# Four graph layers in one kernel: a comparison in another form, and a call moved inside a sum

## The reference

```python
# first layer: graph convolution
deg  = segment_sum(1, dst);  dinv = rsqrt(deg)
msg  = h[src] * dinv[src] * dinv[dst]
x   += h + relu(segment_sum(msg, dst) @ W_gcn @ W1 + b1) @ W2 + b2
# fourth layer: attention on edges, per pair (i, o) of 16 x 16
w_m  = (efeat @ W_msg  + b_msg ).reshape(E, 16, 16)
w_a  = (efeat @ W_attn + b_attn).reshape(E, 16, 16)
e1, e2 = w_m * h[src][:, :, None], w_a * h[src][:, :, None]
attn = exp(e2 - segment_max(e2, dst)) / segment_sum(exp(...), dst)
x   += segment_sum(e1 * attn, dst).sum(axis=1)
```

## Time and profile before

| | us |
|---|---|
| median of three runs | 9471.54 |
| profiled execution | 9465.25 |
| its span | 9463.5 |
| busy TensorE / VectorE | 7645.1 / 7338.7 |
| busy GpSimd / ScalarE | 6896.2 / 4606.7 |

### The profile page before, as it was taken

One profiled execution on the slowest core, in us unless ns is written; L12 is line 12 of the kernel. 1 busy time (PEld: TensorE's weight loads), 2 busy tenths in 40 slices (PEclk: granted clock), 3 DMA queues, 4 the chain that ended last, 5 costly groups with the idle time before them and its releaser, 6 DMA issues. The chain is left out here.

```text
span 9463.5 us, 135509 instructions
## 1 busy us (share of the span) xinstructions
PE 7645.1 (81%) x35152; PEld 4283.9 (45%) x35152; DVE 7338.7 (78%) x11881; ACT 4606.7 (49%) x7496; POOL 6896.2 (73%) x6335
## 2 busy tenths in 40 slices
PE   3777774999999728888888888578888888888884
PEld 3666653555555415555555555333333333333331
DVE  6666653777777738888888888588888998988987
ACT  4666663667667416565655665323333333333333
POOL 6777776766666567777777777378777777777774
PEclk9888886777777659999999999789999999999997
DMA  4222211111111111111111111122222222222223
GB/s 147 55 52 53 55 46 36 42 41 40 42 41 40 34 17 32 31 27 31 31 27 31 31 31 21 18 62 72 77 72 71 72 71 75 75 71 72 71 74 99
DMA packets 498923, 493.19 MB, mean 52 GB/s; under 512 B 180303, under 2 KB 396134, under 8 KB 497959
## 3 DMA queue, kind: packets, MB, share of 16 engines
q1 hardware_dynamic: 298823, 371.60, 11.6%
q0 software_dynamic: 199904, 119.78, 9.1%
HBM read 240.96 MB, written 249.95 MB: 52 GB/s over the span
## 5 line engine op out<-in xcount | busy, mean ns | idle before, releaser
L2485 POOL DMA_INDIRECT attn_got<-tab,attn_line x1760 | 2152.3, 1223 | 648.7 <-issue 511.2
L1945 POOL DMA_INDIRECT sheaf_got<-tab,sheaf_idx x1612 | 1712.7, 1062 | 490.0 <-issue 472.5
L2538 PE MATMUL attn_q<-attn_X,ident 128*128 128x512 f32 x3520 | 1799.3, 658 | 1.8 <-DVE attn_X L2710 1.8
L2034 PE MATMUL sheaf_acc<-sheaf_hot_hi,sheaf_wide 128*128 128x392 bf16 x6696 | 1361.4, 346 | 272.1 <-DVE sheaf_hot_hi L2237 270.2
L1469 POOL DMA_INDIRECT nnconv_got<-tab,nnconv_idx x1116 | 1100.0, 986 | 456.0 <-issue 322.8
L1167 POOL DMA_INDIRECT gcn_got<-tab,gcn_idx x868 | 1018.9, 1174 | 301.4 <-issue 275.4
L2671 DVE TENSOR_TENSOR attn_T<-attn_w,attn_got 128x1024 f32<-128x1024 f32 x880 | 1035.0, 1218 | 246.4 <-PE attn_w L2529 206.6
L2538 PEld LDWEIGHTS attn_q<-attn_X,ident 128*128 128x128 f32 x3520 | 699.9, 210 | 1136.6 <-issue 1136.6
L2615 ACT COPY attn_S<-attn_q 128x512 f32<-128x512 f32 x440 | 255.9, 582 | 1624.4 <-PE attn_q L2545 1624.4
L2034 PEld LDWEIGHTS sheaf_acc<-sheaf_hot_hi,sheaf_wide 128*128 128x128 bf16 x6696 | 657.2, 106 | 809.2 <-issue 481.0
L2529 PE MATMUL attn_w<-src_hi 32*128 32x512 f32 x3520 | 586.5, 738 | 437.6 <-DVE attn_T L2671 436.7
(11 more groups left out here) (502 smaller groups left out, 13931.2 us busy)
## 6 DMA issues: line engine op xcount, KB each, us to landing
sums<-attn_S SPq DMA_DIRECT2D x110, 1024.0 KB, 4.2
tops<-attn_S SPq DMA_DIRECT2D x110, 512.0 KB, 2.9
attn_got<-tab,attn_line POOLq DMA_INDIRECT x1760, 2.6
sheaf_got<-tab,sheaf_idx POOLq DMA_INDIRECT x1612, 2.4
gcn_key<-src_key SPq DMA_DIRECT2D x62, 384.0 KB
gcn_blk<-src_blk SPq DMA_DIRECT2D x62, 384.0 KB
nnconv_got<-tab,nnconv_idx POOLq DMA_INDIRECT x1116, 2.4
nnconv_key<-src_key SPq DMA_DIRECT2D x62, 256.0 KB, 3.1
```

Of the source, the lines that this page charges most:

```text
L1945: e.indirect_dma_start(out=got[at.b][:, j, D:D + T2], out_offset=None, in_=tab[2], in_offset=indices(idx[at.b], j)).then_inc(s_got[half][a ...
L2034: mm = e.matmul(pacc[k][:, 0:HH], wide[at.b][half][:, part, col, :], hot[:, k * HH:(k + 1) * HH], start=False, stop=False, skip_group_chec ...
L2485: e.indirect_dma_start(out=got[at.b][:, 4 * q + n, :], out_offset=None, in_=tab[3], in_offset=indices(ids[:, q, n, :], D + 2)).then_inc(s_ ...
L2538: e.matmul(to, ident[:, :], X[:, q, :, n, :], start=n == 0, stop=False)
```

## The change

A bank of PSUM is set to one at the start of the first convolution, and `chosen` compares with `scalar_tensor_tensor` instead of `tensor_scalar`: the comparison's result is multiplied by that bank. In attention `quad_sum` takes a function that it calls after its third identity matmul; for quad 0 of a block this function is the call of `matrices(at.plus(2), 0)`, which stood behind the whole sum.

```diff
+            pone = ps("gcn_one", [P, 512], banks)
...
                     ch.do(e.memset(pcnt[:, 0:C], 0.0))
+                    ch.do(e.memset(pone[:, :], 1.0))
...
                         for n in range(NC):
-                            hit = e.tensor_scalar(hot[q][:, n, :], key[at.b][:, g, :], key_of[:, n:n + 1], None, ALU.is_equal)
+                            hit = e.scalar_tensor_tensor(out=hot[q][:, n, :], in0=key[at.b][:, g, :], scalar=key_of[:, n:n + 1],
+                                                         in1=pone[:, :], op0=ALU.is_equal, op1=ALU.mult)
                         hit.then_inc(s_hot, 1)
...
-                    def quad_sum(at, q):
+                    def quad_sum(at, q, between=None):
...
                         for n in range(4):
                             e.matmul(to, ident[:, :], X[:, q, :, n, :], start=n == 0, stop=False)
+                            if between and n == 2:
+                                between()
...
-                        quad_sum(at, 0)
-                        if at.k < NBQ - 2:
-                            matrices(at.plus(2), 0)
+                        quad_sum(at, 0, (lambda: matrices(at.plus(2), 0)) if at.k < NBQ - 2 else None)
```

## The result

The kernel after takes 9212.98 us (median of three, 9211.11 to 9216.05) against 9471.54: ratio 0.9727, 95% interval 0.9705 to 0.9749. The profiled execution took 9216.05 us, 249.2 less than the one before; the other 9.4 us of the medians' difference lie in which execution was profiled.

A forecast was written before the change was run, and what follows sets the result against it. GpSimd's gathers bound the first convolution; in attention VectorE and TensorE wait for each other. Profiled 9465.25 us less 73 (first convolution) and 86 (attention) gives 9306, plus 6.3 to the runs' median: 9312 us, range 9260 to 9410.

The forecast's parts named there:

- Who bounds the first convolution, and what the new form costs: First convolution: GpSimd's gathers set the 20.70 us period; new comparisons step 0.66 us, seven take 4.62, 1.76 more.
- The sum there: First convolution: first copy 6.5 us later, then 61 periods of 19.4 us, ending at 1347 against 1420: -73 us.
- The two loops: First convolution, per block after the change: VectorE's loop at 18.9 us and GpSimd's gathers at 19.1 us.
- the surcharge: First convolution: a period of 19.4 us taken, above loops of 18.9 and 19.1, because each perturbs the other.
- Attention's place of the gain and its cap: Attention: matrices 1.77 us earlier remove VectorE's 1.23 us wait; the second matrices cap the period's fall at 0.89 us.
- the slack of 0.89 us: Attention: second matrices usable at 7422.55 us, used by VectorE at 7423.44; all that the period can fall.
- Attention's sum: Attention: 0.8 us taken for each of 108 blocks, -86 us, bounds 0 and 140; slow groups after the idle stretch unchanged.
- GpSimd's 27.6 us in attention as a bound: Attention: GpSimd's instructions with their issue need 27.6 us per block; its pace limits the gain to 1.3 us a block.
- The lock rule: First convolution: skill page's full block of GpSimd beside two-port VectorE; a rival blocking scan and digits had 20.1 us, chance 0.08.
- The range: Whole kernel: 9260 to 9410 us, drawn past the rival in which attention gives nothing (9398 us, chance 0.12).
- the prediction's own bounds: Largest gains allowed per stage: -100 us in the first convolution (period 18.95 us), 140 us in attention (GpSimd's pace).

The follow-up runs named there:

- x8: The kernel after, with three filling matmuls into a bank nobody reads in TensorE's idle stretch in attention; 9198.83 us, ratio 0.9716.
- x12: The kernel before, with one filling matmul in TensorE's idle stretch in attention, order of calls unchanged; 9438.29 us, ratio 0.9967.
- x5: The kernel after, with the moved call one matmul later, after the fourth identity matmul; 9215.65 us, ratio 0.9736.
- x3: The kernel after, with the ones in SBUF and not in a PSUM bank; 9513.49 us, ratio 1.0052.
- x7: The kernel before, with three filling matmuls in TensorE's idle stretch in attention, order of calls unchanged; 9298.22 us, ratio 0.9822.

## Why the prediction was wrong

- *Who bounds the first convolution, and what the new form costs.* Right. The step from one comparison to the next is 658 ns (0.66 taken), seven take 4.70 us, 1.84 more than before (1.76 taken), the first copy comes 6.7 us later (6.5), and gathers beside the new form are at 0.95 us.
- *The sum there.* Wrong in size: -99.5, not -73. "The two loops, 18.9 and 19.1 us, nearly tie, and each perturbs the other, so I take 19.4": they hardly perturb each other; the period is 19.07. Without the surcharge, 61 x 0.33 = 20 us of the 26 missing are there; the rest is the last period, 12.1 us, in which ScalarE, which waited 6.93 us for the last gathers before, finds them done.
- *Attention's place of the gain and its cap.* Right: the wait for the first matrices goes, the slack of 0.89 us limits it, and a like block is 0.82 us shorter. In the kernel after VectorE's second multiplications start 1.31 us after their matrices in the mean, 1.27 being the least; before it was 2.21, so the slack is used up. VectorE's own work is as near: with the clock up (x8) the period is still 27.33 us, against 27.40 in the short blocks of the kernel after.
- *Attention's sum.* This is the step that failed: "TensorE's idle stretch of 3.89 falls to about 3.0 us, still long, so I leave the slow groups after it as they are". They did not stay: blocks with over 6 us at the low clock fell from 43 of 94 to 4 of 98, worth 0.6 us a block, 65 us. It was a term of the sum set to nought without bounds. Of the two misses this is the one that decides: with the first convolution as measured and attention as forecast the time would be some 9285 us, inside the range. Why the second low stretch stays away in this order is open: x12 shows that the idle stretch's length alone doesn't do it, and x5 that the exact place of the call doesn't matter.
- *GpSimd's 27.6 us in attention as a bound.* Wrong: the period went below it, to 27.45. A gather's mean length fell from 1223 to 1178 ns, so such a pace is not a constant of GpSimd; that VectorE's work falls otherwise beside it is the likely reason, not a tested one.
- *The lock rule.* The Trainium skill's page "SBUF — State Buffer", section "Who interferes with whom", puts a full block beside two-port modes, and also between a VectorE instruction with two SBUF inputs and a GpSimd instruction that reads SBUF. Neither the old comparisons, 1.28 us for a gather, nor the kernel after, whose period was 19.07 and not 20.1, show a block over the whole row of instructions. It came in x3, beside an operation with two tensors in SBUF: 5.00 us beside 4.72, for 33 of 552 gathers, while most beside the same comparisons took 1.02 us.
- *The range.* It ended at 9260 for want of a term for the clock. It was also narrower than the prediction's own bounds, -100 and -140 us, which end at 9231; the measured 9213 is below these too, since attention alone gave 153.5 us, more than its bound of 140.

## What to carry to other kernels

Where GpSimd issues gathers all the time, look at where both tensors of VectorE's neighbouring operations lie: the form with a second tensor cost VectorE 0.66 us a comparison instead of 0.41, in a bank or out of it, and still won with that tensor in a bank of PSUM; the same operation with both in SBUF lost all of it. Where TensorE idles once per block, price the slow matmuls after it as a term of their own, with a bound that they go: a few matmuls into a bank that nobody reads test that in one run. Two edits that remove the same wait don't add up, so ask what stands behind it first.

## What the runs showed of the hardware

A gather issued by GpSimd lasted 0.95 us beside comparisons with one tensor in PSUM; with both in SBUF most lasted 1.02 us, and 33 of 552 some 5.0 us, the length of all seven. The digits' operation slowed a gather to 1.8 us with both tensors in SBUF and not at all with one in a bank and in f32, at an equal length of its own (1.48 us). In attention the granted clock alone was worth 170 us: after an idle stretch of 3 to 3.9 us every block ran at 1.2 GHz for at least 3.4 us, and three matmuls of no use in that stretch kept it at 2.4 GHz in 94 of 98 blocks of x7 and in all of x8.
